# Row indices staged by VectorE, gathered tiles released quad by quad, and a VectorE loop that works one quad at a time

## The reference

```python
h  = relu(layernorm(x));  x = x + rgcn2(relu(rgcn1(h)))      # two layers, 10 relations, mean over each relation
h  = relu(layernorm(x));  x = x + rel_conv(h, w_rel[3])       # sum over edges of weight * (h @ W[type])[src]
h  = relu(layernorm(x));  x = x + fc(bn(relu(sage2(sage1(h)))))  # two layers, mean over neighbours
h  = relu(layernorm(x));  x = x + schnet(h)                   # h[dst] * filter(edge features), summed by src
# each of the five layers rgcn1, rgcn2, rel_conv, sage1, sage2 contains
#   agg[n] = sum over edges e with dst[e] == n of w[e] * table[row(src[e], type[e])]
```

## Time and profile before

| what | value |
|---|---|
| time, median of 3 runs | 18440.12 us (18428.23 to 18442.12) |
| span of the profiled execution, first to last instruction | 18422.2 us; no time of its own is given for it, the three runs lie 6 to 20 us above the span |
| POOL busy | 11077.2 us (60%) |
| PE, PEld busy | 8433.5 us (46%), 6706.7 us (36%) |
| DVE busy | 7139.1 us (39%) |
| ACT busy | 2442.5 us (13%) |
| stretch of COUNT and all before the first gather | 0 to 1117 us |
| LOOKUP | 1117 to 3884 us |
| PLAIN 1, 2, 3 | 4171 to 6606, 6806 to 9242, 9458 to 11900 us |
| last PLAIN | 12014 to 14631 us |
| FILTER and the end | 14750 to 18422 us |

### The profile page before, as it was taken

How to read it: one execution, slowest core, us unless ns; L and a number is a source line. 1 busy time by engine, 2 the same in 40 slices (tenths; PEclk the granted TensorE clock), 3 DMA queues, 4 the chain that set the end, 5 groups by cost and what they waited for, 6 DMA issues and landing times. The chain is left out here.

```text
span 18422.2 us, 189911 instructions
## 1 busy us (share of the span) xinstructions
PE 8433.5 (46%) x37745; PEld 6706.7 (36%) x37746; DVE 7139.1 (39%) x33414; ACT 2442.5 (13%) x4374; POOL 11077.2 (60%) x11347
## 2 busy tenths in 40 slices
PE   2464444463333343333343333333333377777777
PEld 1233333333333333333332332322222355555555
DVE  7644444432222232222232222255555534444443
ACT  0120000020000020000020000000000044444443
POOL 0045555636666646666636666566666448888883
PEclk9975555585555565555565555555555567777775
DMA  2131111131111131111121111123333246666665
GB/s 85 64 123 40 40 39 39 40 146 55 45 45 45 45 100 45 45 45 45 45 66 45 45 45 45 49 80 84 83 84 84 73 95 118 118 117 118 117 117 122
DMA packets 981246, 1326.79 MB, mean 72 GB/s; under 512 B 201421, under 2 KB 635620, under 8 KB 981180
## 3 DMA queue, kind: packets, MB, share of 16 engines
q0 software_dynamic: 552016, 851.84, 21.1%
q1 hardware_dynamic: 429208, 474.72, 8.9%
HBM read 992.21 MB, written 333.54 MB: 72 GB/s over the span
## 5 line engine op out<-in xcount | busy, mean ns | idle before, releaser
L588 POOL DMA_INDIRECT rows<-table_dram,row_st x8320 | 8018.1, 964 | 3188.8 <-issue 2894.6
L734 PE MATMUL ps<-tab_s,rows 128*128 128x128 f32 x16640 | 4123.4, 427 | 6939.1 <-DMA rows<-table_dram,row_st 4302.8
L734 PEld LDWEIGHTS ps<-tab_s,rows 128*128 128x128 f32 x16640 | 3604.2, 320 | 7432.5 <-issue 7386.0
L570 POOL DMA_INDIRECT agg_dram<-acc,sum_row x1664 | 2646.9, 1591 | 529.0 <-issue 383.7
L997 DVE TENSOR_TENSOR acc<-ps,acc 128x128 f32 x2080 | 605.5, 291 | 5685.4 <-PE ps L734 4010.6
L1038 DVE TENSOR_SCALAR tab_s<-iota,rw_st 128x128 f32<-128x128 f32 x6656 | 1787.8, 361 | 11.5
L734 PE MATMUL ps<-scratch,tab_s 128*128 128x128 f32 x3328 | 669.0, 366 | 821.8 <-DVE scratch L1182 791.5
L583 POOL COPY row_st<-row_i 128x8 int32 x1040 | 210.5, 202 | 1262.7 <-PE ps L734 1072.4
L734 PEld LDWEIGHTS ps<-scratch,tab_s 128*128 128x128 f32 x3328 | 596.8, 269 | 871.7 <-issue 871.3
L548 POOL DMA_DIRECT2D table_dram<-tab_s x200 | 106.6, 533 | 1179.9 <-ACT tab_s L671 917.4
L635 ACT ACTIVATE yT<-acc 128x512 f32 x75 | 46.9, 626 | 4899.5 <-DVE acc L997 4893.7
(11 more groups left out here) (182 smaller groups left out, 10596.4 us busy)
## 6 DMA issues: line engine op xcount, KB each, us to landing
scratch<-in_src_row SPq DMA_DIRECT2D x832, 256.0 KB
rows<-table_dram,row_st POOLq DMA_INDIRECT x8320
table_dram<-tab_s POOLq DMA_DIRECT2D x200, 640.0 KB, 3.2
scratch<-in_dst_row SPq DMA_DIRECT2D x416, 256.0 KB
scratch<-table_dram SPq DMA_DIRECT2D x416, 64.0 KB
agg_dram<-acc,sum_row POOLq DMA_INDIRECT x1664
scratch<-agg_dram SPq DMA_DIRECT2D x100, 256.0 KB, 3.8
x_dram<-xn_h SPq DMA_DIRECT2D x75, 256.0 KB, 2.4
```

What stands on the lines that cost most here:

```text
L570: pool.indirect_dma_start(agg_dram[j], bass.IndirectOffsetOnAxis(ap=sum_row[:, QUAD * q + j:QUAD * q + j + 1], axis=0), sums[:, q, j * P:( ...
L588: pool.indirect_dma_start(rows[:, u, :], None, table_dram[p["rels"]], bass.IndirectOffsetOnAxis(ap=row_st[:, u:u + 1], axis=0)).then_inc(r ...
L734: pe.matmul(o, lhs[:, u, :], rhs[:, u, :], start=j == 0 or not summed, stop=j == QUAD - 1 or not summed).then_inc(mm_done, 1)
```

## The change

The kernel keeps one bank of 16 gathered tiles. GpSimd no longer copies indices: VectorE copies the 16 indices of the next group into one of two halves of `row_st` (`stage_rows`), once a group, and GpSimd waits for that. GpSimd waits for the products four times a group instead of twice, before each quad, for the same quad of the group before. `mm_done`, `hot_ready` and `add_done` count quads: only the last of four products, one-hots or weighed tiles signals. In PLAIN passes VectorE works quad by quad: it adds quad q of the group before, then builds the one-hots of quad q of this group (`plain_group`), so that the adds of a group lie in the next turn; the last group's adds follow it. In the last PLAIN pass the comparison and masked sums of the quad follow the one-hots. A LOOKUP group keeps its order. Bodies of gathering passes are written out twice for the two halves of `row_st`, with semaphores `row_in` for each. In a PLAIN pass the first index copy comes after `set_windows`.

```diff
--- before.py
+++ after.py
@@ gpsimd, a gathering pass
-                    with pool.Fori(0, ngroups) as g:
+                    def gather(g, bank, i):
                         turn = pool.snap(reps * (k * ngroups) + r * ngroups + g)
-                        used = pool.snap(reps * ntiles + turn * GROUP)
-                        for part in range(2):
-                            pool.wait_ge(mm_done, used + (part + 1) * (GROUP // 2))
-                            us = range(part * (GROUP // 2), (part + 1) * (GROUP // 2))
-                            pool.tensor_copy(row_st[:, us[0]:us[-1] + 1],
-                                             row_i[:, bass.ds(g * GROUP + us[0], GROUP // 2)]).then_inc(row_staged, 1)
-                            pool.wait_ge(row_staged, turn * 2 + (part + 1))
+                        used = pool.snap(reps * (4 * ngroups) + turn * 4)
+                        pool.wait_ge(row_staged, (reps * k + r) * (ngroups + 1) + g + 1)
+                        settle(pool)
+                        for q in range(4):
+                            pool.wait_ge(mm_done, used + (q + 5))
                             settle(pool)
-                            for u in us:
+                            for u in range(QUAD * q, QUAD * (q + 1)):
                                 pool.indirect_dma_start(
-                                    rows[:, u, :], None, table_dram[p["rels"]],
-                                    bass.IndirectOffsetOnAxis(ap=row_st[:, u:u + 1], axis=0)
-                                ).then_inc(row_in[u // QUAD], 16)
+                                    row_banks[bank][:, u, :], None, table_dram[p["rels"]],
+                                    bass.IndirectOffsetOnAxis(ap=row_st[:, bank, u:u + 1], axis=0)
+                                ).then_inc(row_in[bank][q], 16)
+                    groups_by_bank(pool, gather)
@@ the two halves; row_banks = [rows, rows] is one bank of tiles
+        def groups_by_bank(e, body):
+            with e.Fori(0, ngroups // 2) as i:
+                body(i * 2, 0, i)
+                body(i * 2 + 1, 1, i)
+            if ngroups % 2:
+                body(ngroups - 1, 0, ngroups // 2)
@@ tensor, quad_products (mm_done starts at 8 quads)
-                pe.wait_ge(add_done, base + QUAD * (q + 1))
-                pe.wait_ge(hot_ready, base + QUAD * (q + 1))
+                pe.wait_ge(add_done, base + (q + 1))
+                pe.wait_ge(hot_ready, base + (q + 1))
                 for u in range(QUAD * q, QUAD * (q + 1)):
...
-                    pe.matmul(...).then_inc(mm_done, 1)
+                    mm = pe.matmul(...)
+                mm.then_inc(mm_done, 1)
@@ vector, run_pass
+                    def stage_rows(g, bank):
+                        dve.tensor_copy(row_st[:, bank, :], row_i[:, bass.ds(g * GROUP, GROUP)]).then_inc(row_staged, 1)
+                    if kind != COUNT:
+                        dve.wait_ge(rows_ready, sum(q in (0, 2, 3) for q in range(pn)))
+                        stage_rows(0, 0)
...
+                    def lookup_group(g, bank, i):
...
+                        dve.wait_ge(mm_done, base + 8)
+                        stage_rows(g + 1, 1 - bank)
...
+                    def plain_group(g, bank, first, last):
+                        rw = rw_st2[:, bank]
+                        before = None if first else dve.snap(base - 4)
...
+                        for q in range(4):
+                            if first:
+                                dve.wait_ge(mm_done, base + (q + 5))
+                            else:
+                                add_quad(before, win, q, acc, P)
+                            one_hots(q, lambda u: dve.tensor_scalar(hot[:, u, :], iota[:], rw[:, 0, u:u + 1],
+                                                                    rw[:, 1, u:u + 1], ALU.is_equal, ALU.mult))
+                            if finds_dest:
...
+                        stage_rows(g + 1, 1 - bank)
...
+                        if last:
+                            win = windows(dve, g)
+                            for q in range(4):
+                                add_quad(base, win, q, acc, P)
```

More of the change, by code:

```diff
@@ L234, in build @@
         row_staged = sem("row_staged")
-        row_in = [sem(f"row_in{q}") for q in range(4)]
+        row_in = [[sem(f"row_in{b}{q}") for q in range(4)] for b in range(2)]
         rw_staged = sem("rw_staged")
@@ L555, in _ @@
                 wait_stores(pool, k)
-                if PASSES[k + 1] != FILTER:
-                    pool.wait_ge(rows_ready, sum(q in (0, 2, 3) for q in range(k + 1)))
-                else:
+                if PASSES[k + 1] == FILTER:
                     with pool.Fori(0, reps) as r:
@@ L832, in run_pass @@
                                 quad_products(base, q, same, P, msg, summed=False)
+                    if kind in (LOOKUP, PLAIN):
+                        groups_by_bank(pe, group)
+                    else:
+                        with pe.Fori(0, ngroups) as g:
+                            group(g)
             run_pass(0)
@@ L920, in _ @@
             step(dve.memset(wt_deg[:], 0.0))
+            step(dve.memset(row_i[:, ntiles:ntiles + GROUP], 0))
             dve.wait_ge(made, 13)
@@ L1119, in run_pass @@
-                        if kind == LOOKUP:
-                            dve.wait_ge(hot_ready, base + GROUP)
-                            for full, w in ((wt_a, 0), (wt_deg, 1)):
-                                part = full[:, bass.ds(g * GROUP, GROUP)]
-                                dve.tensor_tensor(part, wout_st[:, w, :], part, ALU.add)
+                        dve.tensor_copy(rw_st[:, 1, :], etype[:, bass.ds(g * GROUP, GROUP)]).then_inc(rw_staged, 1)
+                        dve.wait_ge(rw_staged, turn * 2 + 2)
@@ new lines, in run_pass @@
+                    if kind == COUNT:
+                        with dve.Fori(0, ngroups) as g:
+                            count_group(g)
+                    elif kind == LOOKUP:
+                        groups_by_bank(dve, lookup_group)
+                    else:
+                        plain_group(0, 0, True, ngroups == 1)
+                        middle = (ngroups - 2) // 2 if ngroups > 2 else 0
+                        if middle:
+                            with dve.Fori(0, middle) as i:
+                                plain_group(i * 2 + 1, 1, False, False)
+                                plain_group(i * 2 + 2, 0, False, False)
+                        for g in range(1 + 2 * middle, ngroups):
+                            plain_group(g, g % 2, False, g == ngroups - 1)
```

271 lines of the change are left out of this document (137 added, 134 removed).

## The result

The changed kernel takes 18,520.31 us, median of 4 runs (18,511.32 to 18,541.32), the one before 18,441.12 us (18,428.23 to 18,447.26) timed beside it: ratio 1.0045, 95% interval 1.003 to 1.0059. It is slower by 79 us where 1,390 us less were forecast. The experiments ran on other chips, and there the picture splits in two, so I name the chips. This one is A; B to F are five different chips, and whether A is one of them is not known.

The account below looks back on a forecast made before the run. GpSimd's gather stream bounds the PLAIN passes, a VectorE-TensorE chain LOOKUP. 18422 - 990 - 230 - 200 + 30 = 17,032 us of span, hence 17,050 us; 8-in-10 range 16,420 to 17,950.

Parts of the forecast that it names:

- VectorE quad by quad in PLAIN passes: PLAIN 1, 2, 3: one-hots fall between products, so the overlap going with late signals disappears; 330 us a pass won.
- both parts as gone: 148 + 154: PLAIN 1, 2, 3: GpSimd's index copies (148 us a pass) and its waits for products before them (154 us) both vanish.
- PLAIN 1 to 3: Three PLAIN passes: 330 us of the 342 above the gather stream won in each, 990 us together.
- Last PLAIN: Last PLAIN pass: 230 us won, between 0 and 517: the copies (148) and a third of the waits.
- LOOKUP: LOOKUP pass, a chain of VectorE and TensorE: release by quads and fewer hand-over signals win 200 us, bounds 0 and 667.
- Starts: Starts of passes: GpSimd's first gather waits until VectorE has set its windows; 30 us lost in sum.
- COUNT: COUNT and FILTER, no gathers, same order, fewer signals: zero, between -30 and +30 us.
- fewer signals: 12 fewer signals a group from TensorE and 12 from VectorE: zero below; above, their part in lateness already counted.
- Four waits and settles: GpSimd, four waits a group instead of two: zero if met; upper bound 0.51 us each, 212 us a pass.
- rival E: Waits and settles between quads cost 0.51 us each in five passes and eat the copies' gain: 18,476 us; 6%.
- D: Rival, slower: unbroken stream keeps signals late, each quad's new wait met late; decides from 0.8 us a quad, 19,340 us; 7%.
- C: Rival: late state stays in every pass, only the copies' 148 us won in four passes, nothing in LOOKUP: 17,878 us; 20%.

## Why the prediction was wrong

**The step that failed** is the one on *VectorE quad by quad in PLAIN passes*: "The overlap that goes with late signals disappears", and with it "both parts as gone: 148 + 154", 330 us a pass. It rested on two neighbouring groups, and the earlier trace rows. The overlap was a companion, not the cause: on A the adds are late without it (5521.05 above), on D they are prompt with it (4851.91). The passes gained 32, 33 and 45 us on A in place of 330 each.

What goes with late signals is how long the stream of gathers has run. In PLAIN 1 to 3 of the kernel before, every one of the 121 first products that no one-hot overlapped ended 7 to 9 us after a pause of GpSimd (over 1.5 us idle), and none of those groups has a late add. Most of the 191 overlapped ones ended later in the stream, and 34 of those groups have no add over 1 us late either. In PLAIN 1 of the changed kernel, of the products that end 5 to 15 us after gathers resumed 2 of 120 are added over 1 us late, of those that end later 284 of 286; the 10 that end sooner are late too, they started in the pause. The prediction compared the group of the earlier trace rows, just after a pause, with that of the earlier trace rows, whose first product ends 30 us into the stream.

With the distance between gathers raised from 1.26 to 1.65 us in the mean, by waits between them, no signal was late on E; at 1.26, by quads or halves, a group takes 22.9 to 23.1 us and signals are late (by whole groups 24.63, at most 3.4 us late). That a shared thing of limited rate is behind it fits all of this and is not shown. Taking away 1.4 us of copies a group took away pauses, and new ones took their place: GpSimd now waits before 67 of the 415 quads in PLAIN 1, 4.7 us each, and hardly before the others. In the mean that is 0.75, 0.77, 0.63 and 0.70 us by quad. The mean lateness went from 4.0, 4.5, 2.6, 1.0 to 7.4, 7.5, 7.1, 6.6 us by quad.

Term by term, on A and on D:
- *PLAIN 1 to 3*, forecast -990: -109 on A; -555 on D. On D the copies (164 a pass, forecast 148) are confirmed; the 154 us of waits that I added belong to late signals and are not there to be won. Where they are there, this change didn't win them.
- *Last PLAIN*, forecast -230: 0 on A, where its adds are 14 to 17 us late; -199 on D.
- *LOOKUP*, forecast -200: +168 on A, -182 on D. On D and F it is the copies alone, which I did not name as the source. On A, "gathers that don't pause don't end the late state" was written down and could have turned the sign: the earlier release puts the stream under the end of the chain. Release by halves gives back a third on E; the rest is open.
- *Starts*, forecast +30: the gaps between passes grew by 6 us on A and 24 on D.
- *COUNT*, forecast 0: +22 on both to the first gather. 18 of it are the groups, 5.87 to 6.04 us; the other 4 belong to the start of LOOKUP. The add starts 0.222 us behind the product where it started 0.134 us behind it, though only the last of four matmuls signals now. That is against the term "fewer signals", which I put at no cost; which edit adds the 0.09 us was not tried apart.
- *Four waits and settles*, forecast 0 when met: right. The 0.51 us of rival E never shows; D has 0.30 us before each quad.

Of the rivals, D named the place on chip A: the new wait before a quad, met late before one quad in six, at about 0.7 us a quad in the mean where it decides from 0.8. C was right that the late state stays and wrong that the copies are won in it. In the ratio, D's 0.947 lies between the forecast's 0.925 and C's 0.970. On D the direction came out through the copies: the waits priced at 154 us a pass weren't there. That LOOKUP came near there, -182 against -200, is luck, since the reason given was another one.

What the forecast could have seen: the earlier trace rows shows TensorE's signal late to GpSimd too, which has no part in the overlap. And in PLAIN 1 there is the overlap without the lateness, in a timeline of the kernel before on A:
```profile
5110.85 4.36 DVE L1038 TENSOR_SCALAR tab_s<-iota,rw_st 128x128 f32<-128x128 f32 x16
...
5113.05 2.05 PE L734 MATMUL ps<-tab_s,rows 128*128 128x128 f32 x8 [3.83 <-DVE tab_s L1038]
...
5115.23 0.29 DVE L997 TENSOR_TENSOR acc<-ps,acc 128x128 f32 x1
```
The one-hots (to 5115.21) cover the whole product, and the add comes 0.13 us behind it.

**Open.** Whether it is the chip itself or something around it that lasted over all runs made together: all kernels run side by side agreed in it, and B to F were each met once. What gathers and signals share is open too: the rows' traffic and the number of signals don't load it, TensorE's products at most a little; VectorE's instructions were not tried on a chip with late signals. Every timed run here also has a recorded span, 1.7 us shorter than the time itself, so that none shows a run without recording. The Trainium skill, page "NOTIFIC — the notification-queue block", section "Overflow: three behaviours, one of which stalls the engine", says that this block's internal pipeline pushes back on its producers rather than lose a record; lateness for all engines at once would fit that, and no run here shows it.

## What to carry to other kernels

When a stall and its supposed trigger are read from two neighbouring groups, look for the same trigger without the stall (and the stall without it) over the whole pass before it is priced, and ask what else differs between the two groups, here the time since the last pause. A pause that is filled by useless work may still be needed: ask what comes through in it. When a trace shows signals many us late, time the change on several chips before believing either sign; here one program is 5.3% faster or 0.45% slower.

Of the versions tried, the changed kernel is as fast as any on chips with prompt signals (halves in LOOKUP and two banks are within 0.1% of it). On chips with late ones no version that does all the work beat the kernel before.

## What the runs showed of the hardware

- The same kernel before takes 17,187 to 17,211 us on three chips (C, D, F) and 18,276 to 18,441 in three other places (A, B, E), 6 to 7% apart, with prompt and late signals.
- In PLAIN passes with late signals, released by quads, 16 indirect gathers of 16, 64 or 128 rows take 22.9 us alike; where signals are prompt, 18.4, 19.4 and 20.2. Plain transfers take 8.6 us on both.
- In PLAIN 1 of the changed kernel on A the hold-up sets in for products that end 15 us or more after gathers resume, in the kernel before mostly from 30 us on. Held adds mostly start 3 to 5 us after the last gather has ended (median 4.7 and 3.3). DMA completions are not held: products start 1.81 us behind their last gather on A as on D.
- A signal on only the last of four matmuls comes with an add that starts 0.222 us behind it in place of 0.134 in COUNT, on either kind of chip (A, D, F).
